# Context projections in blocks of three token tiles, and a key-bias matmul on 128 rows

## The reference

```python
ctx_txt = context[:, :TEXT_LEN, :]
ctx_img = context[:, TEXT_LEN:, :]
k = (ctx_txt @ Wk).reshape(B, TEXT_LEN, HEADS, DIM_HEAD)
v = (ctx_txt @ Wv).reshape(B, TEXT_LEN, HEADS, DIM_HEAD)
k_ip = (ctx_img @ Wk_ip).reshape(B, Li, HEADS, DIM_HEAD)
v_ip = (ctx_img @ Wv_ip).reshape(B, Li, HEADS, DIM_HEAD)
```

## Time and profile before

| what | value |
|---|---|
| median of 3 runs | 3376.46 us (3371.82 to 3381.22) |
| the profiled execution | 3377.16 us, span 3375.4 us |
| TensorE busy (matmul) | 3161.2 us, 94% |
| VectorE, ScalarE, GpSimd busy | 58%, 49%, 23% |
| projections | first matmul at 23.3 us, last at about 445 us |
| masked attention | scores from 2336.6 us, last value product at about 2471 us |

### The profile page before, as it was taken

The page is one execution under the profiler, slowest core; times in us unless marked ns, Lnnn a source line. Parts: engine busy times, 40 slices in busy tenths (PEclk is TensorE's granted clock), DMA queues, the critical chain, the costliest instruction groups (busy, mean ns, idle before and its releaser), DMA issues. The chain is left out here.

```text
span 3375.4 us, 51188 instructions
## 1 busy us (share of the span) xinstructions
PE 3161.2 (94%) x16792; PEld 2696.3 (80%) x16792; DVE 1962.9 (58%) x3422; ACT 1667.3 (49%) x3204; POOL 789.5 (23%) x881
## 2 busy tenths in 40 slices
PE   7999979999999969999996798997979999999998
PEld 6988969999999958887884576885857888888886
DVE  3245549999999955557888995554752222222211
ACT  3132249999999943336776785564721111111110
POOL 0000038888888830000000200003700000000000
PEclk9999989999999989999997898998989999999999
DMA  6487755555555545556666686444831110001000
GB/s 187 120 253 228 224 171 165 170 177 173 170 165 173 157 150 198 179 172 203 226 218 219 215 265 218 158 161 165 251 116 60 38 35 24 31 26 38 32 25 13
DMA packets 370165, 503.46 MB, mean 149 GB/s; under 512 B 58940, under 2 KB 237420, under 8 KB 366032
## 3 DMA queue, kind: packets, MB, share of 16 engines
q1 hardware_dynamic: 356458, 473.37, 44.6%
q0 software_dynamic: 4768, 18.88, 1.7%
q10 hardware_dynamic: 8720, 8.41, 0.7%
HBM read 292.86 MB, written 174.11 MB: 138 GB/s over the span
## 5 line engine op out<-in xcount | busy, mean ns | idle before, releaser
L2592 DVE SCALAR_TENSOR_TENSOR lf_hT<-lf_hb,lf_hT 128x512 fp32r<-128x512 f32 x128 | 88.5, 691 | 571.6 <-ACT lf_hT L2668 571.6
L2668 ACT ACTIVATE lf_hT<-lf_hb 128x512 fp32r<-128x512 f32 x128 | 76.5, 598 | 669.2 <-PE lf_py L192 639.6
L768 POOL TENSOR_TENSOR at_prob<-at_prob,at_rec 128x308 f32<-128x308 f32 (+1 forms) x256 | 261.3, 1042 | 87.6 <-DVE at_rec L808 87.3
L908 ACT ACTIVATE at_prob<-at_sc,at_nm 128x77 f32<-128x77 f32 (+1 forms) x1024 | 277.6, 385 | 7.3 <-DVE at_nm L795 4.9
L190 PE MATMUL lf_hb<-lf_xT,lf_w 128*128 128x512 f32 x512 | 204.7, 400 | 1.3 <-DVE lf_hT L2592 1.3
L192 PE MATMUL lf_hb<-lf_xT,lf_w 128*128 128x512 f32 x512 | 203.5, 398 | 0.0
L190 PE MATMUL lf_py<-lf_w,lf_hT 128*128 128x512 f32 x512 | 203.1, 397 | 0.0
L192 PE MATMUL lf_py<-lf_w,lf_hT 128*128 128x512 f32 x512 | 203.1, 397 | 0.0
L191 PE MATMUL lf_hb<-lf_xT,lf_w 128*128 128x512 f32 x512 | 203.0, 396 | 0.0
L191 PE MATMUL lf_py<-lf_w,lf_hT 128*128 128x512 f32 x512 | 202.6, 396 | 0.0
L801 DVE TENSOR_REDUCE at_sums<-at_prob 128x4 f32<-128x308 f32 (+1 forms) x256 | 166.1, 676 | 17.7 <-ACT at_prob L908 17.5
(11 more groups left out here) (334 smaller groups left out, 9229.3 us busy)
## 6 DMA issues: line engine op xcount, KB each, us to landing
at_kr<-k_rows SPq DMA_DIRECT2D x256, 128.0 KB, 2.9
at_qs<-at_qst SPq DMA_DIRECT2D x512, 64.0 KB, 2.0
raw_gate<-pg_stage SPq DMA_DIRECT2D x96, 256.0 KB, 2.0
pu_rg<-raw_gate SPq DMA_DIRECT2D x96, 256.0 KB, 3.2
raw_up<-pu_stage SPq DMA_DIRECT2D x96, 256.0 KB, 2.1
om_raw<-raw_up SPq DMA_DIRECT2D x48, 512.0 KB, 4.5
dn_raw<-raw_up SPq DMA_DIRECT2D x48, 512.0 KB, 3.8
xn_parts<-pr_xturned SPq DMA_DIRECT2D x32, 512.0 KB, 5.0
```

The source lines that it names most:

```text
L768: ins = pool.tensor_tensor(prob[:, i, :, lo:hi], prob[:, i, :, lo:hi], rec[:, z, g, :].unsqueeze(2).broadcast_to([P, 2 * NTE, hi - lo]), A ...
L908: ins = act.activation(prob[:, i, m, lo:hi], sc[n % 2][:, m, lo:hi], ACT.Exp, bias=nm[:, n % 2, g, m:m + 1])
L2592: dve.scalar_tensor_tensor(hT[:, i, 1, :], hb[i][:], 0.0, hT[:, i, 0, :].bitcast(F32), ALU.max, ALU.subtract).then_inc(h_done, 1)
L2668: act.activation(hT[:, m % 2, 0, :], hb[m % 2][:], ACT.Relu).then_inc(h_hi, 1)
```

## The change

The blocks are no longer tied to whole batches. The 1232 text tokens of all batches are taken as one row of tokens, cut into blocks of 256, 384, 384 and 208; the 2864 image tokens into 176 and seven times 384. There are still 12 blocks, 4 of text and 8 of image, but three of them (256, 208 and 176) have two tiles and the others three full ones. Key stores now write the columns of a batch that is cut by a block's border as a DMA of their own. The load of the next group of x rows stays 12 jobs behind the start of an image block; since the first image block has 12 jobs, the first of these loads comes at the first job of the block after it.

In the masked attention `trow` and `ones` have 128 rows. GpSimd first sets `trow` to zero, SyncE waits for that before it loads the two rows, and the matmul contracts over 128 rows of which 126 are zero.

```diff
-TB, IB = 4, 2
+TEXT_BLOCKS = (2 * P, 3 * P, 3 * P, B * TEXT - 8 * P)
+IMG_BLOCKS = (B * IMG - 21 * P,) + 7 * (3 * P,)
...
-    for g in range(B // TB):
-        blocks.append(Rows("text", g * TB, TB * TEXT, [((g * TB + i) * S, TEXT) for i in range(TB)]))
-    for g in range(B // IB):
-        blocks.append(Rows("img", g * IB, IB * IMG, [((g * IB + i) * S + TEXT, IMG) for i in range(IB)]))
+    for kind, off, length, sizes in (("text", 0, TEXT, TEXT_BLOCKS), ("img", TEXT, IMG, IMG_BLOCKS)):
+        every = Rows(kind, B * length, [(b * S + off, length) for b in range(B)])
+        lo = 0
+        for n in sizes:
+            blocks.append(Rows(kind, n, [(row, count) for _, row, count in every.pieces(lo, n)]))
+            lo += n
...
-                cols = slice(block.first * S, (block.first + nb) * S)
-                return [(k_d[job[1] * P:(job[1] + 1) * P, cols].rearrange("p (b n) -> p b n", n=S)[:, :, off:off + each],
-                         slot[:, 0:block.n].rearrange("p (b n) -> p b n", n=each))]
+                parts = block.pieces(0, block.n)
+                full = [piece for piece in parts if piece[2] == each]
+                out_ = [(k_d[rows_, row:row + count], slot[:, at:at + count]) for at, row, count in parts if count < each]
+                if full:
+                    at, row, nb = full[0][0], full[0][1], len(full)
+                    off = 0 if block.kind == "text" else TEXT
+                    out_.append((k_d[rows_, row - off:row - off + nb * S].rearrange("p (b n) -> p b n", n=S)[:, :, off:off + each],
+                                 slot[:, at:at + nb * each].rearrange("p (b n) -> p b n", n=each)))
+                return out_
...
-                    if c >= NTX and c + 1 < NBLK and j == first_job[c] + 12:
-                        load_x(c - NTX + 1)
+                    for i in range(NCH - 1):
+                        if j == first_job[NTX + i] + 12:
+                            load_x(i + 1)
...
-        trow = ph.sb("trow", [2, B, S], F32R)
-        ones = ph.sb("ones", [2, P], F32R)
+        trow = ph.sb("trow", [P, B, S], F32R)
+        ones = ph.sb("ones", [P, P], F32R)
...
-            sp.dma_start(trow[:].bitcast(F32), split_d.rearrange("b a s -> a b s")).then_inc(t_ready, 16)
+            sp.wait_ge(trow_cleared, 1)
+            sp.dma_start(trow[0:2].bitcast(F32), split_d.rearrange("b a s -> a b s")).then_inc(t_ready, 16)
...
+            pool.memset(trow[:].rearrange("p b s -> p (b s)").bitcast(F32), 0.0).then_inc(trow_cleared, 1)
             pool.memset(ones[:].bitcast(F32), 1.0).then_inc(ones_made, 1)
```

More of the change, by code:

```diff
@@ L195, with __init__ @@
 IMG = S - TEXT
-TB, IB = 4, 2
+TEXT_BLOCKS = (2 * P, 3 * P, 3 * P, B * TEXT - 8 * P)
+IMG_BLOCKS = (B * IMG - 21 * P,) + 7 * (3 * P,)
 class Rows:
-    def __init__(self, kind, first, n, runs):
-        self.kind, self.first, self.n, self.runs = kind, first, n, runs
+    def __init__(self, kind, n, runs):
+        self.kind, self.n, self.runs = kind, n, runs
         self.tiles = [(lo, min(P, n - lo), max(0, lo + P - n)) for lo in range(0, n, P)]
@@ L219, in context_blocks @@
     blocks = []
-    for g in range(B // TB):
-        blocks.append(Rows("text", g * TB, TB * TEXT, [((g * TB + i) * S, TEXT) for i in range(TB)]))
-    for g in range(B // IB):
-        blocks.append(Rows("img", g * IB, IB * IMG, [((g * IB + i) * S + TEXT, IMG) for i in range(IB)]))
+    for kind, off, length, sizes in (("text", 0, TEXT, TEXT_BLOCKS), ("img", TEXT, IMG, IMG_BLOCKS)):
[4 more added lines that the diff above has]
+            lo += n
+        assert lo == every.n
     return blocks
@@ L246, in project_context @@
     blocks = context_blocks()
-    NBLK, NTX = len(blocks), B // TB
+    NBLK, NTX = len(blocks), len(TEXT_BLOCKS)
     jobs = [(c, job) for c, block in enumerate(blocks) for job in jobs_of_block(block)]
@@ L318, in stores @@
                 each = TEXT if block.kind == "text" else IMG
-                off, nb = (0 if block.kind == "text" else TEXT), block.n // each
-                cols = slice(block.first * S, (block.first + nb) * S)
-                return [(k_d[job[1] * P:(job[1] + 1) * P, cols].rearrange("p (b n) -> p b n", n=S)[:, :, off:off + each],
-                         slot[:, 0:block.n].rearrange("p (b n) -> p b n", n=each))]
+                rows_ = slice(job[1] * P, (job[1] + 1) * P)
+                parts = block.pieces(0, block.n)
[7 more added lines that the diff above has]
+                return out_
             lo, count, skip = block.tiles[job[1]]
@@ L2025, in masked_attention @@
         r_ready, c_ready = [ph.sem(f"r_ready{i}") for i in range(NR)], [ph.sem(f"c_ready{i}") for i in range(NC)]
-        m_ready, traw_ready, t_high, t_low, t_stored, t_ready, ones_made = (
-            ph.sem(n) for n in ("m_ready", "traw_ready", "t_high", "t_low", "t_stored", "t_ready", "ones_made"))
+        m_ready, traw_ready, t_high, t_low, t_stored, t_ready, ones_made, trow_cleared = (
+            ph.sem(n) for n in ("m_ready", "traw_ready", "t_high", "t_low", "t_stored", "t_ready", "ones_made", "trow_cleared"))
         stat_done, mv_ready, var_ready, rstd_ready, shift_ready, xn_ready, spacer_d, spacer_p, spacer_a = (
```

## The result

The changed kernel takes 3405.85 us (median of 4 runs, 3402.82 to 3410.65) beside 3377.47 us for the kernel before on the same chip: 0.9% slower, ratio 1.009 with a 95% interval from 1.0077 to 1.0102. The profiled execution has a span of 3406.9 us. Forecast were 3348 us, so 58 us are to be found. They lie in one stage. TensorE's last matmul of the projections starts at 489.7 us, where before it was 444.9, and the rest of the kernel is not slower: the span is 31.5 us longer, with 44.8 us lost in the projections and some 13 us won behind them.

The account below looks back on a forecast made before the run. TensorE was taken as the bound in projections and masked attention. Part A -19.5 and Part B -10 sum to -29.5 us: 3377.2 to 3347.7, so 3348 us, own range 3341 to 3355 (60%), wider range 3339 to 3370.

Parts of the forecast that it names:

- Stores ... Taken at 0, hidden by six staging slots: Projections: more key and value stores, key stores from 96 to 248, cost 0; SyncE keeps ahead, staging slots hide them.
- Stores collide: Rival, projections: 10240 added packets paid on the path, 32 us at most; half gives 3364, all 3380; 9%.
- The start: Start of projections: two tiles in block 0 bring earlier matmuls and load, no 1.85 us idle; -4 us, bounds 0 and -6.
- the start gives nothing: Rival, start of projections: a weight load takes the place of the wait; 3352 us, 10%.
- Value jobs: Projections: six fewer jobs of 12 matmuls at 0.231 us each, all on the path; -16.6 us.
- turns: Projections: three fewer turns of four transposes, 0.4 us each, one counted in the start; two give -0.8 us.
- near 425: Sign, end of projections: the last value matmul comes near 425 us instead of 445.
- Part A: Projections: token tiles from 36 to 33, jobs from 168 to 162, blocks stay 12; -19.5 us in all.
- Key jobs: Projections: same columns in new block widths, narrow matmuls taken at 0.099 us; +1.4 us, bounds -0 and +5.
- The rival of plain fp32's pace: Projections: fp32r matmuls below 256 columns fall to plain fp32's pace, 43 us added; 3391 us, 12%.
- Block 5: Projections: x-row load issued later, statistics due two jobs later, VectorE may stand 4 us; +0.5 us, bounds 0 and +3.
- Part B: Masked attention: key bias matmul on 128 rows instead of 2, 14 batches at 0.70 us; -10 us, bounds 0 and -13.

Follow-up runs that it names:

- e12: e11, with only runs that put over 17 rows on a DMA engine cut: 3342.55 us, ratio 0.99 to the kernel before.
- e2: Changed kernel, each run of value stores and row loads issued as a multiple of 16 rows and the rest: 3353.63 us, ratio 0.9933.
- e11: e2 with the pieces of the image weights due every second job instead of every job: 3348.13 us, ratio 0.9917.
- e6: Kernel before, with each value store of 102 rows cut into 94 and 8 rows: 3384.23 us, ratio 1.0026.
- e1: Kernel before, with only the key bias change (trow and ones on 128 rows, memset, SyncE's wait): 3366.5 us, ratio 0.997.
- e10: e2 with the old key bias on 2 rows: 3361.54 us, ratio 0.9957 to the kernel before.

## Why the prediction was wrong

It failed at one step: "Stores ... Taken at 0, hidden by six staging slots". The stores and loads were counted, in issues (0.38 us each) and in packets, and neither count is what hurt: 248 key stores at a median of 0.43 us are harmless in e12. What was not looked at is the number of rows in each value store and row load, and so the number of DMA engines that share it. The new blocks made runs that go to one or two engines; behind them single issues stand for up to 10.1 us, which six slots don't hide. The step is worth 52 us (changed kernel against e2); the other 6 of the 58 go, as far as e11 shows, with the late weight below.

- The rival "Stores collide" named the right place and the wrong mechanism: full engines, at most 32 us, bounded from above at no change. The engines were emptier than before, and its bound did not hold. A mark of the true cause stood in its own argument: it priced a packet as if spread over 16 engines.
- How stalls of SyncE become TensorE's time: from the first image matmul (145.1 us, 138.9 in e12) to the end of the projections (490.0, 424.6) are 344.9 us instead of 285.7 in e12, so 59 are lost. 45.0 us are TensorE's waits on VectorE, of which e12 has 2.4. The other 17 or so go with the granted clock, 0.96 and 0.92 where e12 has 1.00 (at most 155 x 0.04 + 192 x 0.08 = 22 us, an estimate from those two rows): after an idle TensorE runs at the lower of its two levels for a while, as at 62.4 us in e2. The prediction's six slots put the wait off, but don't take it away: at 403 to 411 us SyncE stands and TensorE runs 8.00 of 8.00 us, and then it waits 6.7 us, to 422.0. What they do cover is most of the stalls of 2 to 3 us in e6.
- The start, "-4; bounds 0 (a weight load is late instead...)": the first part of the step held and more, the first matmul at 19.48 us instead of the forecast 22.0. The forecast took off the third turn alone (1.3 us); the fourth piece of Wk, which ScalarE and VectorE split ahead of block 0's copies, also came sooner: ScalarE began on it at 15.91 us instead of 18.36, with two loads fewer issued ahead of it. The weight that is late instead came as the rival "the start gives nothing" had it, with another price: an idle of 5.7 us and 1.75 us of half clock behind it in e2, more than the start gains. It lies 40 us behind the start, on VectorE's queue, which the prediction had not followed so far. The shorter wait in e11 shows it.
- Value jobs (-16.6) and turns: in e12, without the stalls, the last matmul of the projections starts at 424.2 us; forecast was "near 425", before 445. So the sum of Part A is right in size where nothing stands in its way. That it is so close is in part luck: in e12 the first matmul comes 2.0 us sooner than forecast (20.02), and the narrow matmuls below take 2.3 us more. 552 value matmuls on image weights remain of 576, as counted.
- Key jobs: 0.099 us for a narrow matmul was too low. Both widths, 176 and 208 columns, take 0.111 us. That is 96 x 2 x 0.012 = 2.3 us more than taken, within the bounds. The Trainium skill (TensorE: Matmul & The Clock Gate, LDWEIGHTS) has a weight load take its columns over 1.2 GHz, by which we estimate 107 ns for 128 columns; against what the prediction held, the 0.111 here goes with the page, though the one-column row of 0.083 does not. That the weight load is what holds both widths at 0.111 us is not shown. The rival of plain fp32's pace (0.295 and 0.349) fell.
- Block 5, "+0.5; bounds 0 and +3": TensorE waits 3.3 us in e2 for the normalised x rows, 2.9 of them in block 5; before it was 1.0 in all. That is near the upper bound.
- Part B, -10: measured -9.6 alone (e1) and -7.9 on top of the blocks (e10 to e2). The memset takes 3.5 us on GpSimd (3.6 taken), and GpSimd idles 1.5 us before its next work (1.3 forecast).
- The sum -29.5: e12 is 32.6 us below before (3375.18), with the two edits that free the change, of which the forecast had neither. The forecast was that of a kernel whose transfers are spread like the old ones.

## What to carry to other kernels

When blocks are cut to a size that suits TensorE, factor the row count of every DMA that follows from it: a run of 127 or 101 rows works on one engine in sixteen, and its queue holds up everything that is issued behind it. Price a transfer by the rows on its fullest engine against the time until the next one, not by packets and not by the number of DMAs (here, with rows of 2 KB, 17 rows on the fullest engine cost nothing, and 47 in 16 stores 13.7 us); issuing the multiple of 16 and the rest apart is nearly free. A waiting TensorE with a DMA share that falls is a sign of it in a profile, and a stretch with a share of 0.07 or 0.08 is little more than one engine at work.

## What was not expected of the hardware

- One issue on SyncE can take 10.1 us. It stands with the DMA behind the bad one, or the next but one, and not with the DMA that causes it, so the view of the store line accuses the key stores.
- The price is steep: 96 rows and 6 cost nothing, 94 and 8 cost 13.7 us more than those, 101 and 1 cost 79 us more, for 16 stores of a kernel of 3.4 ms.
- In stretches with a share of 0.07 and 0.08, little more than one of the 16 DMA engines, 28 and 30 GB/s were moved.
- fp32r matmuls of 176 and of 208 columns both take 0.111 us, where 256 columns take 0.120.
